# A chunked recurrence on one core: the state summed in PSUM, copied by ScalarE, and read for the queries behind the update

## The chip, the cores and the metric

One core of a Trainium2 chip runs the whole program. The metric is the device time of one execution in microseconds (us). Each kernel is executed several times and the median is given; one further execution is profiled, and its trace is what the rows below are from.

## The reference

The input x is 2048 tokens by 512 features in float32. It goes through an attention-like layer and then a feed-forward layer, each with a residual and a LayerNorm.

```python
def step(S, inp):                       # one chunk of 16 tokens, 16 heads of 32
    qi, ki, vi, ei = inp
    kh = ki @ S                         # keys read the state
    target = vi - ki
    kh_hat = (kh - mean(kh)) * rsqrt(var(kh) + EPS)
    g = w * kh_hat + b - target
    gw = g * w
    v_new = (gw - mean(gw) - kh_hat * mean(gw * kh_hat)) * rstd
    A = where(tri, qi @ ki.T, 0) * ei
    qh = qi @ S - A @ v_new             # queries read the state of before the chunk
    o = qi + ln(qh, w, b)
    S = S - (ki * ei).T @ v_new         # the state of the next chunk
    return S, o
...
x = x + layernorm(attn(layernorm(x)))   # attn: q, k, v, beta, gate projections, the scan, Wo
x = x + layernorm(ffn(layernorm(x)))    # ffn: weights rounded to fp8 values, silu(gate) * up, down
```

The scan is a chain of 128 steps; everything else can be done beside it. B and T are laid out as one sequence of 2048 tokens, so there are 128 chunks in all.

## The kernel before

The 2048 tokens are 16 tiles of 128 tokens. A tile has 8 chunks; in a chunk both halves of the heads are worked together. Every engine has its own program, and `timeline(body, prologue)` runs a prologue and then `body(t)` for t = 0 to NT + DRAIN - 1. In body(t) the scan is at tile t, the projections (`prep_...`) are made for tile t + 1, the LayerNorm of the input for t + 2, the output normalisation (`post_...`) for t - 1, the residual and second LayerNorm (`tail_...`) for t - 2, and the feed-forward layer runs in pairs of tiles behind that (`ffn_...`, `fin_...`). The order on each engine is written out by hand: for each chunk j = 0 to 7 there is scan work, then background work assigned to that j. Engines wait on semaphores, always in order.

One chunk of the scan, before:

- TensorE (`read_state`): four products `KAv[...] = bdk * SQv` (L431, "kh"), which give the keys' read of the state and, from 16 more columns, the queries against the keys. Then four products for the queries' read of the state into `QH` (L440, "qs"). Then TensorE's background of this j.
- VectorE (`scan_front`, `scan_back`): from `bn_stats` (L1140) over some ten small steps to `VX` (L1176). GpSimd gives it rho (L904, a power of two columns) on the way.
- TensorE (`write_state`): `dS[...] = bdkr * VX` (L454, "upd"), then `QH += atb * VX` (L461, "qa"), then a second piece of background.
- VectorE (`scan_state`): `S = S + dS` (L1183). This waits for upd. VectorE's background of this j stands behind it, apart from one operation that stands between VX and it.
- ScalarE: `chunk_q` (L720) puts the queries of the next chunk beside the state in `SQ`, once kh has read it; `take_qh` (L729) copies QH out. ScalarE's background stands before `take_qh`, and some behind it.

The next kh waits for `S` and for `chunk_q`. KA and dS lie in PSUM bank 0, QH in bank 1.

The feed-forward weights come in 36 blocks of 128x512 (256 KB), "units". They are rounded on VectorE in the chunks 0 to 24: `magic` (L1273, L1276), and one chunk later `shift` (L1280) and `quantize` (L1284). Chunk c takes the units c\*3//2 to (c + 1)\*3//2 - 1, so even chunks begin one unit and odd chunks two. The units are staged in three buffers, used in turn:

```python
for u in last_units(t, j):          # SP: the units that this chunk quantizes
    if u + 3 < UNITS:
        sp.wait_ge(s_quant, u + 1)
        stage(u + 3)
...
for u in last_units(t, j):          # VectorE, at the end of each chunk's background
    shift(u)
    quantize(u)
for u in units(t, j):
    magic(u)                        # waits for the landing of unit u
```

VectorE's background in the scan's chunk j, with s = t % 2, besides these: j 0 `tail_x1` (s = 1); j 1 `prep_thR`, `tail_x1` (s = 0), `ffn_f`; j 2 `post_n`, `pair_xl` (s = 1), `prep_kss`, `ffn_fl`, `x_stats`; j 3 `post_o`, `prep_qR`, `post_og`; j 4 `post_oss`, `prep_kn`, `prep_d`, `ffn_f`; j 5 `prep_kR`, `fin_y` twice (s = 1); j 6 `post_on`, `post_ogT`, `prep_bx`, `fin_stats` twice (s = 1); j 7 `prep_rR`, `prep_eta` (waits for TensorE's `prep_brow`, L419), `ffn_f`, `tail_stats`, `fin_out` twice (s = 1).

The prologue prepares tile 0 in the same order and in the same two PSUM banks as every other tile: q, k, then a wait for all eleven small tensors, v, keys turned, beta, gate, and at the end VectorE scales Wo by norm_w (four operations of 128x512).

Of the kernel before, what the change touches and what calls it, by code (L numbers as in the profile page):

```python
# [9 lines left out]
I32 = mybir.dt.int32  # L10
# [52 lines left out]

def begun(n):

    return not isinstance(n, int) or n >= 0


def build(nc, x, wq, wk, wv, wo, wbeta, wg1, wg2, norm_w, ln_w, ln_b, gate_w, up_w, down_w,
# [15 lines left out]
    with ctx:  # L85
# [11 lines left out]
        nw, gs, us = sb("nw", KD), sb("gs", MI), sb("us", MI)  # L97
# [38 lines left out]
        yb = [sb(f"yb{k}", D) for k in range(2)]  # L136
        xn2 = [sb(f"xn2{s}", D) for s in range(2)]
# [21 lines left out]
        QH = bank[1]  # L159
# [8 lines left out]
        s_setup = sem("s_setup")  # L168
# [11 lines left out]
        prep_v = Steps(sem("prep_v"), "kss qR kn d kR bx rR em er eM thR")  # L180
        prep_a = Steps(sem("prep_a"), "xnT q ksq qT g1 beta BDk rT th")
        prep_t = Steps(sem("prep_t"), "xnT q k qT v kT2 kT1 g1 beta dT gate cen brow")
        prep_g = Steps(sem("prep_g"), "kse rk qb b1")
# [3 lines left out]
        scan_t = Steps(sem("scan_t"), "kh qs upd qa")  # L187
        scan_v = Steps(sem("scan_v"), "bn p m at u g0 g1 s0 s1 t0 t1 vx S")
        scan_g = Steps(sem("scan_g"), "rho rho2 re")
        scan_a = Steps(sem("scan_a"), "qh")  # L190
# [49 lines left out]
        DRAIN = 4  # L240
# [48 lines left out]

        block = ctx.enter_context(nc.Block())  # L290

        @block.sync
        def _(sp):
            def stage(u):
                src = (gate_w, up_w, down_w)[u % 3]
                sp.dma_start(wst[u % 3][:, :], src[:, u // 3 * D:(u // 3 + 1) * D]).then_inc(s_stage[u % 3], 16)
# [3 lines left out]
            sp.dma_start(Wq[:, :].rearrange("p (k n) -> p k n", k=KD),  # L300
                         wq.rearrange("(k p) n -> p k n", p=P)).then_inc(s_wq, 16)
            for dst, src in ((Wg1, wg1), (Wb, wbeta)):
                sp.dma_start(dst[:, :].rearrange("p (k n) -> p k n", k=KD),
                             src.rearrange("(k p) n -> p k n", p=P)).then_inc(s_small, 16)
            for dst, src, s in ((Wk, wk, s_wk), (Wv, wv, s_wv)):
                sp.dma_start(dst[:, :].rearrange("p (k n) -> p k n", k=KD),
                             src.rearrange("(k p) n -> p k n", p=P)).then_inc(s, 16)
            for dst, src in ((Wg2, wg2), (nw, norm_w), (gs, gate_s), (us, up_s), (wR, ln_w), (bR, ln_b),
                             (wF, ln_wf), (bF, ln_bf)):
                sp.dma_start(dst[:, :], src).then_inc(s_small, 16)  # L310
            sp.dma_start(ds[:, :], down_s.partition_broadcast(P)).then_inc(s_small, 16)
            sp.wait_ge(norm_a.sem, norm_a.at("xn", 0))
            sp.dma_start(xt[:, :], x_t[1]).then_inc(s_x, 16)
            sp.dma_start(Wo[:, :].rearrange("p (k n) -> p k n", k=KD),
                         wo.rearrange("(k p) n -> p k n", p=P)).then_inc(s_wo, 16)
            for u in range(3):
                stage(u)

            def body(t, s, h):
# [16 lines left out]
                if s and is_pair(h - 2):  # L336
                    for k in range(2):
                        n = 2 * (h - 2) + k
                        sp.wait_ge(fin_v.sem, fin_v.at(f"out{k}", h - 2))
                        sp.dma_start(out_t[n], x1[n % 4][:, :]).then_inc(s_out[n % 4], 16)  # L340
# [6 lines left out]
        def _(pe):  # L347
# [13 lines left out]
            def prep_xnT(t):  # L361
                pe.wait_ge(norm_a.sem, norm_a.at("xn", t))
                if begun(t - 1):
                    pe.wait_ge(prep_v.sem, prep_v.at("em", t - 1))
                turn(PA[0], xn, prep_t.one("xnT"))

            def prep_q(t):
                pe.wait_ge(prep_a.sem, prep_a.at("xnT", t))
                proj(PA[0][:, :], Wq, D).then_inc(*prep_t.one("q"))

            def prep_beta(t):
                pe.wait_ge(prep_v.sem, prep_v.at("kR", t))
# [10 lines left out]
            def prep_k(t):  # L383
                pe.wait_ge(prep_a.sem, prep_a.at("q", t))
# [27 lines left out]
            def prep_cen(t):  # L412

                pe.wait_ge(prep_a.sem, prep_a.at("rT", t))
                mm(PA[0][:, :], cst[:, C_CEN:C_CEN + P], rT[:, :], start=True, stop=True).then_inc(*prep_t.one("cen"))  # L415

            def prep_brow(t):
                pe.wait_ge(prep_v.sem, prep_v.at("rR", t))
                mm(PA[0][:, 0:P], cst[:, C_REP:C_REP + P], bx[:, :], start=True, stop=True).then_inc(*prep_t.one("brow"))  # L419

            def read_state(n, j, s):

                c = NC * n + j
                if j == 0:
                    pe.wait_ge(prep_a.sem, prep_a.at("BDk", n))
# [3 lines left out]
                for gh in range(2):  # L429
                    for gp in range(2):  # L430
                        ins = mm(KAv[gp * 64:(gp + 1) * 64, gh, 0:48], bdk(s)[:, gh * NC + j, gp, :],  # L431
                                 SQv[:, 2 * gh + gp, :], start=True, stop=True, skip_group_check=True)
# [1037 lines left out]
```

## Time and profile before

| | |
|---|---|
| median of 3 runs | 997.14 us (993.86 to 998.51) |
| the profiled execution | 994.7 us |
| its span, first to last instruction | 992.9 us |
| TensorE busy | 865.5 us (87%) |
| VectorE busy | 697.9 us (70%) |
| ScalarE, GpSimd busy | 456.5 us (46%), 447.1 us (45%) |
| mean granted TensorE clock | 0.916 |

Busy time is the time that an engine's instructions cover. In the rows PE is TensorE, DVE VectorE, ACT ScalarE, POOL GpSimd and SP the queue that issues the transfers; L1183 is a line of the kernel. A buffer is named by the tensor that owns it, so that S appears as SQ, KA, QH and dS as bank, and the staging buffers as x and xn.

### The profile page before, as it was taken

How to read it: one execution, taken by the hardware profiler on the slowest of the kernel's cores; microseconds unless marked ns; L12 is line 12 of the kernel's file. 1: busy time of each engine (PE TensorE's matmuls, PEld its weight loads, DVE VectorE, ACT ScalarE, POOL GpSimd, SP SyncE). 2: the span in 40 equal slices, each digit the busy share in tenths (PEclk: the TensorE clock that was granted, in tenths of full speed). 3: DMA queues.
4: the chain of work that ended last, by engine and by line, in shares of the span. 5: the costliest groups of instructions: out<-in, count | busy, mean ns of one | idle time of the engine just before them, and what ended most of it. 6: DMA issues, size and time to landing. Idle time of an engine off the chain costs nothing.

```text
span 992.9 us, 21210 instructions
## 1 busy us (share of the span) xinstructions
PE 865.5 (87%) x7488; PEld 621.6 (63%) x7488; DVE 697.9 (70%) x2746; ACT 456.5 (46%) x1250; POOL 447.1 (45%) x828
## 2 busy tenths in 40 slices
PE   4676757677999999999999999999999999979895
PEld 2334435344667767676767676767676676767694
DVE  1477898888767777767776777767776777676442
ACT  3434324334454646464555565554556364542322
POOL 3231351533546454545463554545454545446312
PEclk9776766767999999999999999999999999989998
DMA  7011112111000001000000001000100010001000
GB/s 254 11 44 54 54 53 65 54 43 43 2 23 2 23 1 44 2 23 1 23 23 23 1 2 44 2 22 2 44 2 22 2 44 1 2 1 44 1 22 21
DMA packets 16714, 28.37 MB, mean 29 GB/s; under 512 B 3520, under 2 KB 3520, under 8 KB 16608
## 3 DMA queue, kind: packets, MB, share of 16 engines
q1 hardware_dynamic: 16608, 27.02, 8.5%
q8 instruction: 59, 0.97, 0.4%
q14 instruction: 47, 0.39, 0.1%
HBM read 22.82 MB, written 4.19 MB: 27 GB/s over the span
## 4 chain that ended last, share of the span: by engine, by line
PE 64%; DVE 20%; POOL 7%; issue 4%; ACT 2%; SPq 1%; DMA 1%; POOLq 0%; DVEq 0%; ACTq 0%
PE bank L352 14%; PE bank L489 13%; PE bank L520 8%; PE bank L473 6%; PE bank L454 5%; PE bank L461 3%; POOL rho L904 3%; PE bank L431 3%; PE bank L358 3%; PE bank L440 2%; PE bank L409 2%; PE bank L374 2%; PE bank L415 2%; DVE work L1167 2%; DVE work L1171 1%
## 5 line engine op out<-in xcount | busy, mean ns | idle before, releaser
L904 POOL TENSOR_TENSOR rho<-sy,cst 128x2 f32<-128x2 f32 x128 | 89.8, 702 | 390.6 <-DVE sy L1140 390.6
L454 PE MATMUL bank<-VX,BDkR 128*64 128x64 f32 x1024 | 61.3, 244 | 84.0 <-DVE VX L1176 83.5
L729 ACT ACTIVATE qhR<-bank 128x64 f32<-128x64 f32 x128 | 28.4, 222 | 224.9 <-PE bank L461 221.4
L454 PEld LDWEIGHTS bank<-VX,BDkR 128*64 128x64 f32 x1024 | 43.6, 145 | 137.3 <-issue 75.1
L1183 DVE TENSOR_TENSOR SQ<-SQ,bank 128x128 f32<-128x128 f32 x128 | 36.8, 288 | 94.9 <-PE bank L454 94.1
L520 PE MATMUL bank<-DW,fh 128*128 128x512 f32 x192 | 87.7, 457 | 1.9 <-DVE fl L1248 1.9
L688 ACT ACTIVATE BDkR<-kR,cst 128x128 f32<-128x128 f32 x256 | 81.1, 392 | 0.0
L520 PE MATMUL bank<-DW,fl 128*128 128x512 f32 x192 | 76.4, 398 | 0.0
L1162 DVE SCALAR_TENSOR_TENSOR work<-work,rho,rR 128x32 f32<-128x32 f32 x256 | 53.1, 249 | 31.2 <-POOL rho L904 30.5
L352 PE MATMUL bank<-Wv,xnT 128*128 128x512 f32 x128 | 66.8, 670 | 2.5 <-DVE qR L1085 2.5
L489 PE MATMUL bank<-xh,GW 128*128 128x256 f32 x384 | 66.0, 295 | 2.7 <-DVE xl L1233 2.4
L352 PE MATMUL bank<-Wq,xnT 128*128 128x512 f32 x128 | 67.3, 673 | 0.8 <-ACT xnT L623 0.8
L431 PEld LDWEIGHTS bank<-SQ,BDk 128*64 128x64 f32 x1024 | 44.6, 149 | 36.8 <-issue 28.1
L489 PE MATMUL bank<-xh,UW 128*128 128x256 f32 x384 | 66.8, 297 | 0.7 <-DVE f L1242 0.7
L985 POOL TENSOR_TENSOR fl<-f,fh 128x512 fp32r<-128x512 f32 x32 | 45.7, 1429 | 45.1 <-ACT fh L623 29.3
L473 PE MATMUL bank<-Wo,o 128*128 128x512 f32 x128 | 62.6, 634 | 2.6 <-DVE o L1215 2.6
L431 PE MATMUL bank<-SQ,BDk 128*64 128x48 f32 x1024 | 60.5, 243 | 4.4 <-DVE Wo L1396 3.1
L674 ACT ACTIVATE BDk<-bank 32x256 f32<-32x256 f32 x128 | 48.0, 375 | 34.2 <-PE bank L358 32.7
L489 PE MATMUL bank<-xl,GW 128*128 128x256 f32 x384 | 62.8, 287 | 0.0
L489 PE MATMUL bank<-xl,UW 128*128 128x256 f32 x384 | 62.8, 287 | 0.0
L1140 DVE BATCH_NORM_STATS2 sy<-bank 128x6 f32<-128x68 f32 x128 | 28.9, 226 | 47.5 <-PE bank L431 47.4
L720 ACT ACTIVATE SQ<-qT 128x64 f32<-128x64 f32 x128 | 32.3, 253 | 61.6 <-PE bank L431 61.1
(149 smaller groups left out, 2202.6 us busy)
## 6 DMA issues: line engine op xcount, KB each, us to landing
xt<-in_x SPq DMA_DIRECT2D x16, 256.0 KB, 2.7
x<-in_x SPq DMA_DIRECT2D x16, 256.0 KB, 2.9
out<-x SPq DMA_DIRECT2D x16, 256.0 KB, 2.1
x<-in_gate_w SPq DMA_DIRECT2D x12, 256.0 KB, 2.6
x<-in_up_w SPq DMA_DIRECT2D x12, 256.0 KB, 2.6
xn<-in_down_w SPq DMA_DIRECT2D x12, 256.0 KB, 2.8
Wq<-in_wq SPq DMA_DIRECT2D x1, 1024.0 KB, 8.4
Wk<-in_wk SPq DMA_DIRECT2D x1, 1024.0 KB, 10.0
```

Of the source, the lines that this page charges most:

```text
L352: ins = mm(dst, xnT[:, k * P:(k + 1) * P], W[:, k * n:(k + 1) * n], start=(k == 0), stop=(k == KD - 1))
L431: ins = mm(KAv[gp * 64:(gp + 1) * 64, gh, 0:48], bdk(s)[:, gh * NC + j, gp, :], SQv[:, 2 * gh + gp, :], start=True, stop=True, skip_group_ ...
L454: ins = mm(dS[p, e], bdkr[:, gh, j % 4, p], VX[:, e], start=True, stop=True, skip_group_check=True)
L473: ins = mm(PA[1][:, :], ogT[:, g * P:(g + 1) * P], Wo[:, g * D:(g + 1) * D], start=(g == 0), stop=(g == 3))
L489: ins = mm(b[:, q * PAIR:(q + 1) * PAIR], W[:, k * I + m * P:k * I + (m + 1) * P], part[:, k * PAIR:(k + 1) * PAIR], start=(part is xh and ...
L520: ins = mm(Y[k][:, :], part[:, q * PAIR + k * P:q * PAIR + (k + 1) * P], DW[:, m * D:(m + 1) * D], start=(m == 0 and part is fh), stop=(m ...
L674: ins = fn(bdk(s)[q, :, gp, own(h)], PA[1][p:p + 32, 256 * a:256 * a + 256].rearrange("p (m c) -> p m c", c=CH), ACT.Copy)
L688: ins = fn(bdkr[:, :, place, h * DH:(h + 1) * DH], kR[:, :].rearrange("p (gh j e) -> p gh j e", gh=2, e=DH)[:, :, js], ACT.Identity, scale ...
L904: tt(dst, src, cst[:, C_NH:C_NH + n], ALU.pow).then_inc(*one)
L985: tt(fl[:, :], f[:, :], fh[:, :].bitcast(F32), ALU.subtract).then_inc(*low_g.one("fl"))
L1162: stt(out=g2(g)[:, gh], in0=g2(u)[:, gh], scalar=rho[:, gh:gh + 1], in1=r_j[:, gh, :], op0=ALU.mult, op1=ALU.add).then_inc(*scan_v.one(f"g ...
L1183: tt(S, S, dS.rearrange("p (g e) -> p g e", e=DH), ALU.add).then_inc(*scan_v.one("S"))
```

## The change

It does these things.

1. The state is summed in PSUM: upd accumulates onto dS over all 128 chunks (only the very first clears it), `scan_state` is gone from VectorE, and ScalarE copies dS (128x128) into one of two SBUF buffers in turn (`take_S`).
2. The queries' read of the state (qs) moves from behind kh to behind upd. Both KA and QH now lie in bank 1, and kh waits for `take_qh` of the chunk before, which stands behind `take_S` on ScalarE.
3. On ScalarE `prep_q`, `prep_ksq` and `prep_th` move from before the two copies to behind them.
4. VectorE's background is dealt anew: `x_stats` from j 2 to j 1 (s = 1) or j 5 (s = 0); `tail_stats` for odd tiles and the second `fin_out` from j 7 to j 0 of the next tile; GpSimd's `tail_ra` (s = 0) from j 0 to j 1, `norm_rs` from j 3 to j 2 or j 6.
5. The units are staged in two buffers instead of three, and yb shares xn2's buffers.
6. A new prologue: k before q, beta, v and q into banks of their own, each wait for just what is needed, memsets behind the first normalisation, Wo's scaling on GpSimd, half of one copy and r's scaling on VectorE. Transfers are issued in the new order.
7. The prep stages have one semaphore for each step (`Each`), so that their order may differ. DRAIN is 5 instead of 4, for the moved `fin_out`.

```diff
-        SQ = sb("SQ", 4 * 48)
+        SQ = [sb(f"SQ{n}", 4 * 48) for n in range(2)]
...
-        wst = [x1[2], x1[3], xn2[1]]
-        wmg = [yb[0], f]
+        wst = [x1[2], x1[3]]
+        wmg = [xn2[1], f]
...
-        KA, dS = bank[0][:, 0:100], bank[0][:, 128:256]
+        dS = bank[0][:, 0:128]
+        KA, QH = bank[1][:, 0:100], bank[1][:, 128:192]
...
                     for u in last_units(t, j):
-                        if u + 3 < UNITS:
+                        if u + 2 < UNITS:
                             sp.wait_ge(s_quant, u + 1)
-                            stage(u + 3)
+                            stage(u + 2)
...
             def read_state(n, j, s):
                 pe.wait_ge(chunk_a.sem, chunk_a.at("q", c))
-                if begun(c - 1):
-                    pe.wait_ge(scan_v.sem, scan_v.at("S", c - 1))
+                if begun(c - 1):
+                    pe.wait_ge(scan_a.sem, scan_a.at("qh", c - 1))
...
             def write_state(n, j, s):
-                        ins = mm(dS[p, e], bdkr[:, gh, j % 4, p], VX[:, e], start=True, stop=True,
+                        ins = mm(dS[p, e], bdkr[:, gh, j % 4, p], VX[:, e], start=(c == 0 and gh == 0), stop=True,
                 ins.then_inc(*scan_t.one("upd"))
+                ...                                   # the four qs products, from S[c % 2]
+                ins.then_inc(*scan_t.one("qs"))
...
+            def take_S(n, j):
+                act.wait_ge(scan_t.sem, scan_t.at("upd", NC * n + j))
+                fn(S[(j + 1) % 2], dS.rearrange("p (g e) -> p g e", e=DH), ACT.Copy).then_inc(*scan_a.one("S"))
...
                     if scan:
+                        take_S(t, j)
                         take_qh(t, j, s)
...
+                    if j == 1 and prep:
+                        prep_q(t + 1)
+                    if j == 2 and prep:
+                        prep_ksq(t + 1)
...
-            def scan_state(n, j):
-                c = NC * n + j
-                dve.wait_ge(scan_t.sem, scan_t.at("upd", c))
-                tt(S, S, dS.rearrange("p (g e) -> p g e", e=DH), ALU.add).then_inc(*scan_v.one("S"))
...
             def magic(u):
-                dve.wait_ge(s_stage[u % 3], 16 * (u // 3 + 1))
+                dve.wait_ge(s_stage[u % 2], 16 * (u // 2 + 1))
...
             def prologue():                           # VectorE, the end
                 prep_eta(0, 0, Y[0])
                 prep_rR(0, 0, Y[1])
                 prep_qR(0, 0, G)
                 prep_thR(0, 0)
-                for g in range(KD):
-                    ins = ts(Wo[:, e], Wo[:, e], nw[:, g:g + 1], KAPPA, ALU.mult, ALU.mult)
```

## Rows read from the trace of the kernel before

**Rows 1.** The page, busy time, share of the span, instructions of each engine

```profile
PE 865.5 (87%) x7488; PEld 621.6 (63%) x7488; DVE 697.9 (70%) x2746; ACT 456.5 (46%) x1250; POOL 447.1 (45%) x828
```

**Rows 2.** Windows: busy us of PE, PEld, DVE, ACT, POOL, then clock, DMA

```profile
43.00:229.00 186.00, 130.72 (x1023) 82.69 (x1024) 157.23 (x557) 65.43 (x195) 61.75 (x114) 0.68 0.18 55
...
283.00:861.00 578.00, 560.52 (x5144) 405.14 (x5144) 421.11 (x1773) 308.25 (x855) 298.87 (x553) 0.99 0.05 15
...
861.00:906.00 45.00, 37.52 (x375) 30.47 (x373) 34.55 (x154) 15.79 (x45) 21.53 (x42) 0.89 0.01 1
...
906.00:993.00 87.00, 70.23 (x449) 61.51 (x448) 35.19 (x73) 24.99 (x46) 27.58 (x50) 0.92 0.07 25
```

**Rows 3.** Waits of DVE, 43 to 240 us: us in total, times, longest

```profile
DVE SQ L1183 <- PE bank L454: 14.8, 21, 2.6
...
DVE sy L1140 <- PE bank L431: 2.8, 4, 0.9
```

**Rows 4.** Waits of PE, 43 to 240 us

```profile
PE bank L454 <- DVE VX L1176: 58.3, 15, 6.2
```

**Rows 5.** Timeline of DVE in chunks 8 and 9: start, us, instruction, idle before

```profile
108.88 0.29 DVE L1183 TENSOR_TENSOR SQ<-SQ,bank 128x128 f32<-128x128 f32 x1 [0.28 <-PE bank L454]
109.08 0.68 DVE L1280 TENSOR_TENSOR x<-x,yb 128x512 f32<-128x512 f32 x1
109.80 0.69 DVE L1284 TENSOR_TENSOR UW<-x,yb 128x512 fp32r<-128x512 f32 x1
...
111.74 0.42 DVE L1273 TENSOR_SCALAR yb<-x 128x512 int32<-128x512 int32 x1
...
116.55 0.69 DVE L1284 TENSOR_TENSOR GW<-x,yb 128x512 fp32r<-128x512 f32 x1
...
117.96 0.42 DVE L1273 TENSOR_SCALAR yb<-xn 128x512 int32<-128x512 int32 x1
```

**Rows 6.** Timeline of SP in chunk 9

```profile
117.27 0.33 SPq L296 DMA_DIRECT2D x<-in_gate_w  x1
```

**Rows 7.** DMA issues: KB each, median us from issue to landing

```profile
x<-in_gate_w SPq DMA_DIRECT2D x12, 256.0 KB, 2.6
...
xn<-in_down_w SPq DMA_DIRECT2D x12, 256.0 KB, 2.8
```

**Rows 8.** Timeline of ACT in chunk 10 (j 2 of tile 1)

```profile
120.65 0.60 ACT L650 ACTIVATE xn_dv_rT<-bank 128x512 f32<-128x512 f32 x1 [3.85 <-PE bank L352]
122.29 0.22 ACT L729 ACTIVATE qhR<-bank 128x64 f32<-128x64 f32 x1 [1.05 <-PE bank L461]
```

**Rows 9.** The chain that ended last, in the prologue: start, us, what

```profile
13.13 4.72 DMA ds<-in_down_s
```

**Rows 10.** Timeline of the prologue and of the first chunk

```profile
10.35 5.28 PE L352 MATMUL bank<-Wq,xnT 128*128 128x512 f32 x8 [0.78 <-ACT xnT L623]
...
23.31 2.91 POOL L904 TENSOR_TENSOR rk<-kss,cst 128x16 f32<-128x16 f32 x1
...
41.63 1.63 DVE L1396 TENSOR_SCALAR Wo<-Wo,nw 128x512 f32<-128x512 f32 x4
...
44.13 0.24 DVE L1140 BATCH_NORM_STATS2 sy<-bank 128x6 f32<-128x68 f32 x1 [0.87 <-PE bank L431]
```

**Rows 11.** Timeline of POOL and DVE behind the scan

```profile
918.07 1.30 POOL L980 TENSOR_TENSOR o<-o,wK 128x512 f32<-128x512 f32 x1
...
918.09 1.82 DVE L1248 TENSOR_TENSOR fl<-f,fh 128x512 fp32r<-128x512 f32 x1
```

**Rows 12.** Timeline of PE, tile 6 j 0 and tile 7 j 3

```profile
392.75 0.45 PE L454 MATMUL bank<-VX,BDkR 128*64 128x64 f32 x8 [1.39 <-DVE VX L1176]
...
463.98 0.45 PE L454 MATMUL bank<-VX,BDkR 128*64 128x64 f32 x8 [1.30 <-DVE VX L1176]
```

**Rows 13.** Timeline of DVE, tile 6 j 7 to tile 7 j 0

```profile
438.48 0.29 DVE L1121 TENSOR_TENSOR work<-bank,cst 128x128 f32<-128x128 f32 x1 [1.40 <-PE bank L419]
...
440.85 0.20 DVE L1140 BATCH_NORM_STATS2 sy<-bank 128x6 f32<-128x68 f32 x1
```

More of the change, by code:

```diff
@@ L61, in at, with __init__, one @@
         return len(self.names) * n + self.names.index(name) + 1
+class Each:
+    def __init__(self, sem, stage, names):
+        self.sems = {name: sem(f"{stage}_{name}") for name in names.split()}
+    def one(self, name):
+        return self.sems[name], 1
+    def at(self, name, n):
+        return self.sems[name], n + 1
 def begun(n):
@@ L135, in build @@
         f = sb("f", D)
-        yb = [sb(f"yb{k}", D) for k in range(2)]
-        xn2 = [sb(f"xn2{s}", D) for s in range(2)]
+        xn2 = yb = [sb(f"xn2{s}", D) for s in range(2)]
         norms = ("p", "a", "f", "y0", "y1")
@@ L179, in build @@
         norm_a = Steps(sem("norm_a"), "xn")
[L180 to L183, printed above, removed]
+        prep_v = Each(sem, "prep_v", "kss qR kn d kR bx rR em er eM thR")
+        prep_a = Each(sem, "prep_a", "xnT q ksq qT g1 beta BDk rT th")
+        prep_t = Each(sem, "prep_t", "xnT q k qT v kT2 kT1 g1 beta dT gate cen brow")
+        root_g = Steps(sem("root_g"), "kse rk")
+        prep_g = Each(sem, "prep_g", "qb b1")
         diag_a = Steps(sem("diag_a"), "q0 q1")
@@ L332, in body @@
                     for u in last_units(t, j):
-                        if u + 3 < UNITS:
+                        if u + 2 < UNITS:
                             sp.wait_ge(s_quant, u + 1)
-                            stage(u + 3)
[L336 to L340, printed above, removed]
+                            stage(u + 2)
+                if is_pair(h - 3 + s):
+                    p, k = h - 3 + s, 1 - s
+                    n = 2 * p + k
+                    sp.wait_ge(fin_v.sem, fin_v.at(f"out{k}", p))
+                    sp.dma_start(out_t[n], x1[n % 4][:, :]).then_inc(s_out[n % 4], 16)
             timeline(body, lambda: None)
@@ L614, in prologue @@
-                pe.wait_ge(s_setup, 4)
+                pe.wait_ge(norm_a.sem, norm_a.at("xn", 0))
+                turn(PA[0], xn, prep_t.one("xnT"))
+                pe.wait_ge(*prep_a.at("xnT", 0))
+                pe.wait_ge(s_wk, 16)
+                proj(PA[1][:, :], Wk, D).then_inc(*prep_t.one("k"))
+                pe.wait_ge(s_early, 16 * 2)
+                for k in range(KD):
+                    ins = mm(Y[0][0:DG, 0:P], Wg1[:, k * DG:(k + 1) * DG], xnT[:, k * P:(k + 1) * P],
+                             start=(k == 0), stop=(k == KD - 1))
@@ new lines, in prologue @@
+                ins.then_inc(*prep_t.one("g1"))
+                proj(Y[0][:, P:P + H], Wb, H).then_inc(*prep_t.one("beta"))
+                pe.wait_ge(s_wv, 16)
+                proj(Y[1][:, :], Wv, D).then_inc(*prep_t.one("v"))
+                pe.wait_ge(s_wq, 16)
+                proj(G[:, :], Wq, D, (0, 1))
+                pe.wait_ge(*prep_v.at("kn", 0))
+                turn(PA[0], kn, prep_t.one("kT2"))
+                turn(PA[1], kn, prep_t.one("kT1"))
+                pe.wait_ge(*prep_v.at("d", 0))
@@ new lines, in prologue @@
+                turn(U4, dv, prep_t.one("dT"))
+                proj(G[:, :], Wq, D, (2, 3)).then_inc(*prep_t.one("q"))
+                pe.wait_ge(*prep_v.at("bx", 0))
+                mm(Y[0][:, 0:P], cst[:, C_REP:C_REP + P], bx[:, :], start=True, stop=True).then_inc(*prep_t.one("brow"))
+                pe.wait_ge(*prep_a.at("rT", 0))
+                mm(Y[1][:, :], cst[:, C_CEN:C_CEN + P], rT[:, :], start=True, stop=True).then_inc(*prep_t.one("cen"))
+                pe.wait_ge(*prep_a.at("q", 0))
@@ L616, in _ @@
+                turn(G, qtok, prep_t.one("qT"))
+                pe.wait_ge(s_small, 16 * 6)
+                for m in range(4):
+                    ins = mm(U4[:, m * P:(m + 1) * P], Wg2[:, m * P:(m + 1) * P], g1T[:, :], start=True, stop=True)
+                ins.then_inc(*prep_t.one("gate"))
+                pe.wait_ge(s_half, 1)
+                pe.wait_ge(s_mask, 2)
             timeline(body, prologue)
@@ L1312, in body @@
                         prep_rR(t + 1, o)
-                    if scan:
-                        scan_state(t, j)
-                    if j == 0 and tail and s:
-                        tail_x1(t - 2)
+                    if j == 0:
+                        if tail and s:
+                            tail_x1(t - 2)
+                        if tail and not s:
+                            tail_stats(t - 2)
+                        if not s and is_pair(h - 3):
+                            fin_out(h - 3, 1)
                     if j == 1:
```

335 lines of the change are left out of this document (177 added, 158 removed).

## The prediction

> **What bounds the kernel now.** I read the page's busy times first: TensorE 87%, VectorE 70% [rows 1]. Such a share is a mean over stages, so the windows came next [rows 2], and they show four. From 43 to 229 us (tiles 0 to 2, while the weights are rounded) VectorE is busy 157 of 186 us and TensorE 131 at a clock of 0.68: VectorE bounds. From 283 to 861 us (tiles 4 to 14) TensorE is busy 560.5 of 578 us: it bounds, and only 17.5 us can be won there. From 861 to 906 us (tile 15, nothing left to project) TensorE has 7.5 us without work: the chain through the chunk bounds. From 906 us on there is no scan. Ahead of all this stands a prologue of 44 us. The waits agree: between 43 and 240 us VectorE waits 14.8 us for upd in front of the state's add and 2.8 us for kh in front of `bn_stats` [rows 3], while TensorE waits 58.3 us for VX [rows 4]. The timeline of one even and one odd chunk then shows VectorE's instructions back to back [rows 5].
>
> **The change, part by part, against the profiled span of 992.9 us.**
>
> *Staging in two buffers.* In which chunk is a unit loaded, and in which is it needed? With two buffers unit u + 2 is issued when unit u is quantized. In an odd chunk VectorE quantizes one unit, 3k, and then begins 3k + 1 and 3k + 2; the transfer of 3k + 2 is issued only at the end of that same quantize. In an even chunk it quantizes 3k + 1 and 3k + 2 and begins 3k + 3, whose transfer is issued behind the first of these. Before, with three buffers, each had a whole chunk's time. Quantize starts at 116.55, the transfer is issued at 117.27, 0.72 later [rows 5, 6], and lands 2.6 to 2.8 us after its issue [rows 7]; with 0.04 for the wake, `magic` can start some 3.4 us behind the quantize's start. Without the wait it would start sooner: in the odd chunk the unit in question is the second begun, at 117.96, 1.41 behind the quantize; in the even chunk it is the one begun at 111.74, 1.94 behind the quantize at 109.80 [rows 5]. So VectorE stands 2.05 us in each odd chunk (down or the like, 2.7 to 2.8) and 1.42 in each even one. Units 2, 5, ... 35 are twelve odd cases, 3, 6, ... 33 eleven even ones: 12 x 2.05 + 11 x 1.42 = **+40.2**. It lies on VectorE, in order, right in front of the next `scan_front`. Bounds: 0 if VectorE would wait for kh there anyway, but that wait is 2.8 us in all [rows 3]; 23 x 2.1 = 48 at most.
>
> *`scan_state` gone.* VectorE no longer waits for upd in front of its background. In tiles 0 to 2 that frees the 14.8 and 2.8 us of waits and, from start to start, 0.20 us for each of 24 adds [rows 3, 5]: 22.4. Against that stand three things that are late next. `prep_kss` needs `prep_ksq`, which ScalarE now does behind upd, qs, qa and both copies. Before, it started at 120.65, ahead of `take_qh` at 122.29 [rows 8], and kss followed the add without a wait. Now it starts after it, and kss some 2 us later than VectorE can take it: three tiles, 6 us. `prep_eta` needs brow, which comes behind upd, qs and qa: VectorE reaches it an add earlier and it comes the length of qs later, some 0.8 us, three times, 2.4. And chunk 0, with only one `magic` behind VX, waits 2.2 us for the next kh. Together -22.4 + 10.6 = **-12**. Bounds: everything freed, -28.8, the whole idle time of VectorE in this stretch [rows 2]; nothing, 0.
>
> *Prologue.* Before, k's product waits till 17.9 us for the last of eleven small tensors [rows 9], and v's waits in one bank for k's; GpSimd's power over 16 columns is 2.91, and Wo's scaling, 1.63, is the last thing ahead of the scan [rows 10]. Now k starts where q did, at 10.35, and ends near 15.6, as q did with 5.28; square, sum and power take 0.6, 0.7 and 3.1 (here and behind, each step has the length that the same step has in the prologue before), so rk is there at 20.3 while beta's and v's products end near 21. Then kn 22.5, keys turned 24.1, rest of q 26.5, brow and cen 28.1, q turned 28.7, four copies and the queries' columns on ScalarE 30.6. Two sets of diagonal copies (1.67 and 1.28) and tanh follow at 34.1, thR's turn on VectorE 34.8, then `bn_stats`, which was at 44.13 [rows 10]: **-9**. GpSimd's four products of 512 columns at 1.3 [rows 11] run from 23 to 28.7, beside this. Bounds -5 (a landing 4 us later, each step behind it) and -12.
>
> *Steady tiles.* Here TensorE waits in four chunks of a pair of tiles: about 1.4 and 0.6 in the even tile, 0.1 and 1.3 in the odd one (two of them in [rows 12]). All come from VectorE's background being late at the end of a chunk. At j 7 it isn't the add that makes it late: VectorE waits 1.4 us for brow at 438.48, then works till `bn_stats` at 440.85 [rows 13], and brow follows TensorE's order as before. What helps in front of even tiles is the moved `tail_stats` and `fin_out` (0.8 + 0.65): `bn_stats` 1.4 earlier. At j 2 the new wait for ksq makes VectorE late by about 1 us for j 3, against 1.3 and 2.2 before. But qs no longer fills TensorE's time until VX, so in each chunk where TensorE waits for VX its 0.35 us is added. Per pair: j 0 even -1.0, j 3 even 0, j 0 odd +0.35, j 3 odd -0.75: -1.4. 5.5 pairs: -7.7, and -1.3 for stretches of low clock that followed the longest waits: **-9**. Elsewhere qs is only moved within TensorE's own work. Bounds: -17.5, all of the idle time [rows 2], and +6 if the qs term comes alone.
>
> *The copies.* A ScalarE copy of 64 columns is 0.22 us and 512 columns are 0.60 [rows 8], so 128 take about 0.28. Behind upd come qs, qa (0.35 each) and TensorE's second background (0.5 to 1.4 in full tiles), so both copies are hidden. Where there is none, in tiles 0 to 2 and tile 15, kh now waits 0.3 for `take_qh`, hidden in the former by VectorE.
>
> *Tile 15.* Here TensorE waits for VX in five or six chunks; each grows by qs 0.35 and some by the copy's 0.3, less what VectorE saves: **+2**, between 0 and 4. Behind it: the same work, 0; the moved `fin_out` waits for the same things.
>
> *A lock between VectorE and GpSimd.* At 918.09 a VectorE operation with two SBUF inputs takes 1.82 us, beside GpSimd's 1.30 of 512 columns that began 0.02 before it [rows 11]. GpSimd's big operations wait for VX and used to run beside the add's wait; now they start with VectorE's background. At j 6 `prep_bx` would stand about 0.7 us, in each of 12 tiles. I count 0, since VectorE there has about that much time to spare before TensorE's next kh; on the path it is 8 us. The Trainium skill (SBUF — State Buffer, section "SBUF: two separate sides") says that the pair is held exclusively for a whole instruction and the loser blocks; by that rule the sum has these 8 us wherever the two meet on the path, and the trace agrees with the rule in this one case: 1.82 where such operations take 0.68 or 0.69 [rows 5].
>
> Sum: +40.2 - 12 - 9 - 9 + 2 = +12.2; 992.9 becomes 1005.1, and 994.7 with what lies around it 1006.9. The runs' median is 2.4 above the profiled execution, which would give 1009.3. I take **1008**.
>
> **Rivals.** (a) *The landing is hidden.* VectorE's wait for a unit replaces a wait that it would have for TensorE, so that the 40 us cost little. For it: TensorE's low clock in tiles 0 to 2 makes its work long, 131 of 186 us [rows 2]. Against: TensorE waits 58 us for VX there [rows 4]. Fully hidden it gives 968. It decides once the waits cost under 28 us, 1.2 for each of 23. Chance 0.13. (b) *The steady tiles give all their idle time back*, because ksq and the rest come in time, and VectorE's relief is nearer 20 than 12: -8 and -8, 992. Chance 0.19. (c) *The new copies or GpSimd hold the chain*: ScalarE does its background before `take_S`, and a late copy delays kh; at 0.3 us in half the chunks, or the 8 us of the lock and a cold TensorE during the longer waits, +10 to +14: 1020. Chance 0.13. (d) My case, 1000 to 1016: 0.55.
>
> **How the numbers follow.** 0.5% is 5 us, about what a measurement of this kernel can tell from no change. Slower by more than that: (c) and nearly all of (d): 0.66. Same: half of (b) and some of (d), 0.15. Faster: (a), and the rest of (b), 0.19. For 8 in 10 the range must take in (b) and (c) and leave (a) out: 985 to 1021; my own case alone is 1000 to 1016.
>
> **What would show it.** VectorE idle in front of `magic` (L1273 before), ended by a DMA, 23 times and some 40 us in all; if it is under 20, the first step is wrong. The first `bn_stats` near 35 us. Window of tiles 0 to 2 about 28 us longer. VectorE waiting for ksq about 1.5 us at j 2. TensorE's waits for VX in tiles 4 to 14 about 14 to 17 us still; if they are near 0, (b). ScalarE's `take_S` starting later than 0.3 us behind upd in more than a few chunks, with kh behind it: (c).

## The result and the profile after

The changed kernel takes 1000.3 us (median of 14 runs, 998.2 to 1003.3), the kernel before, in the same sessions, 995.1 (14 runs): a ratio of 1.0051, 95% interval 1.0038 to 1.0063. The change costs 0.5%. I had predicted slower, by 1.1% (997.1 to 1008, or 10.9 us; the medians differ by 5.2). The profiled execution took 1002.5 us, its span 1000.7.

The table goes by five stretches. Their borders are the first `bn_stats` and the first kh product of tiles 3, 4 and 15, read from the timelines of both kernels (before: 44.13, 229.27, 282.95 and 861.24).

| stretch | before | after | difference | predicted |
|---|---|---|---|---|
| start to first `bn_stats` | 44.1 | 34.6 | -9.6 | -9 |
| from there to tile 3 (weights rounded) | 185.1 | 212.9 | +27.8 | +40.2 - 12 = +28.2 |
| tile 3 | 53.7 | 55.7 | +2.0 | 0 |
| tiles 4 to 14 | 578.3 | 565.9 | -12.4 | -9 |
| tile 15 and behind the scan | 131.7 | 131.7 | 0.0 | +2 |
| span | 992.9 | 1000.7 | +7.8 | +12.2 |

The borders after, from TensorE's timeline (start, us, instruction); the second and third have 565.9 us between them:

```profile
247.49 0.44 PE L453 MATMUL bank<-SQ,BDk 128*64 128x48 f32 x8
...
303.17 0.44 PE L453 MATMUL bank<-SQ,BDk 128*64 128x48 f32 x8
...
869.08 0.44 PE L453 MATMUL bank<-SQ,BDk 128*64 128x48 f32 x8
```

The page after, busy times, to be read against [rows 1]: VectorE has lost 26 us of work (the 128 adds), ScalarE has 26 more, and TensorE has 7 less.

```profile
PE 858.4 (86%) x7480; PEld 616.3 (62%) x7480; DVE 672.1 (67%) x2623; ACT 482.3 (48%) x1370; POOL 449.7 (45%) x832
```

The windows after, in the columns of [rows 2]:

```profile
34.50:247.50 213.00, 133.55 (x1018) 83.25 (x1018) 152.31 (x533) 71.45 (x220) 59.61 (x114) 0.65 0.16 46
303.50:869.00 565.50, 552.98 (x5140) 399.86 (x5136) 402.21 (x1685) 327.55 (x943) 298.91 (x553) 1.00 0.05 16
869.00:916.00 47.00, 37.96 (x391) 30.95 (x390) 34.62 (x150) 18.22 (x53) 23.01 (x47) 0.89 0.01 2
916.00:1001.00 85.00, 68.08 (x432) 59.63 (x430) 32.85 (x69) 24.33 (x46) 26.84 (x45) 0.92 0.08 25
```

In tiles 0 to 2 no engine is near full any more: VectorE is busy 152 of 213 us, TensorE 134, at a granted clock of 0.65 (1 is 2.4 GHz, 0.5 is 1.2 GHz; a figure between them is a mean over time). VectorE's waits over the whole span, the four ended by a landing and three others, and below them those of TensorE from 34.5 to 247.5 us:

```profile
DVE sy L1197 <- PE bank L453: 90.7, 68, 3.6
DVE work L1178 <- PE bank L441: 35.0, 15, 2.7
DVE kss L1126 <- ACT xn_dv_rT L690: 32.0, 15, 2.8
...
DVE f L1329 <- DMA x<-in_down_w: 13.4, 6, 3.3
DVE xn L1329 <- DMA x<-in_down_w: 11.7, 6, 2.1
...
DVE f L1329 <- DMA x<-in_gate_w: 8.5, 6, 1.8
DVE xn L1329 <- DMA x<-in_gate_w: 6.7, 5, 1.4
```

```profile
PE bank L467 <- DVE VX L1233: 71.3, 18, 7.9
PE bank L453 <- ACT qhR L769: 6.0, 12, 1.5
```

The four DMA lines add up to 40.3 us in 23 waits; 40.2 in 23 was forecast. One wait of 2.2 us falls in tile 3, the other 38.1 us in tiles 0 to 2. (TensorE's wait for VX was 58.3 us in [rows 4], which reach into tile 3, and 52.2 in tiles 0 to 2 alone, against the 71.3 here.) VectorE's timeline in an odd and in an even chunk shows how each arises:

```profile
117.02 0.69 DVE L1340 TENSOR_TENSOR GW<-x,xn 128x512 fp32r<-128x512 f32 x1
117.63 0.42 DVE L1329 TENSOR_SCALAR f<-x 128x512 int32<-128x512 int32 x1
...
120.41 0.43 DVE L1329 TENSOR_SCALAR xn<-x 128x512 int32<-128x512 int32 x1 [1.89 <-DMA x<-in_down_w]
...
127.54 0.69 DVE L1340 TENSOR_TENSOR UW<-x,f 128x512 fp32r<-128x512 f32 x1
...
130.87 0.43 DVE L1329 TENSOR_SCALAR f<-x 128x512 int32<-128x512 int32 x1 [1.31 <-DMA x<-in_gate_w]
```

From the quantize that frees the buffer to the `magic` that waits for it are 3.39 and 3.33 us; "some 3.4" was forecast.

### The profile page after: what moved, and what is told of

Its sections match the earlier page's. It is cut to its first block, busy times and chain, and to the rows that moved or that the text cites. A ratio compares the mean times of both kernels' runs of the same rounds, so it can differ in the third digit from the quotient of the medians.

```text
span 1000.7 us, 21166 instructions
## 1 busy us (share of the span) xinstructions
PE 858.4 (86%) x7480; PEld 616.3 (62%) x7480; DVE 672.1 (67%) x2623; ACT 482.3 (48%) x1370; POOL 449.7 (45%) x832
## 4 chain that ended last, share of the span: by engine, by line
PE 61%; DVE 18%; POOL 7%; DMA 7%; ACT 4%; issue 3%; POOLq 0%; SPq 0%; ACTq 0%; DVEq 0%
PE bank L374 15%; PE bank L511 11%; PE bank L542 8%; PE bank L495 5%; PE bank L467 5%; PE bank L481 4%; POOL rho L952 3%; DMA x<-in_down_w 3%; PE bank L380 3%; DMA x<-in_gate_w 3%; PE bank L453 2%; PE bank L474 2%; DVE work L1224 2%; PE bank L437 1%; DVE work L1228 1%
## 5 line engine op out<-in xcount | busy, mean ns | idle before, releaser
L762 ACT ACTIVATE SQ<-bank 128x128 f32<-128x128 f32 x128 | 35.2, 275 | 229.9 <-PE bank L467 229.7
L467 PEld LDWEIGHTS bank<-VX,BDkR 128*64 128x64 f32 x1024 | 44.0, 146 | 151.0 <-issue 81.4
L374 PE MATMUL bank<-Wk,xnT 128*128 128x512 f32 x128 | 60.9, 620 | 2.3 <-DMA Wk<-in_wk 2.3
```

The costliest lines, as they stand in the source:

```text
L374: ins = mm(dst, xnT[:, k * P:(k + 1) * P], W[:, k * n:(k + 1) * n], start=(k == 0), stop=(k == KD - 1))
L467: ins = mm(dS[p, e], bdkr[:, gh, j % 4, p], VX[:, e], start=(c == 0 and gh == 0), stop=True, skip_group_check=True)
```

## The experiments

Eleven kernels ran. e1, e3, e5, e7 and e9 are built on the changed kernel, e2 and e11 on the one before; e4 joins e1 and e3, and e6, e8 and e10 are built on e4. e1 to e4 were timed on one chip, e5 to e8 on a second and e9 to e11 on a third, each time beside the kernel before (994.7 to 996.0 there), and the ratio is to that. The last three columns are stretches of the table above, from the timeline of each kernel's one profiled execution.

| kernel | median | ratio (95%) | first `bn_stats` to tile 3 | tile 3 | tiles 4 to 14 |
|---|---|---|---|---|---|
| before | 995 | 1 | 185.1 | 53.7 | 578.3 |
| after | 1000.3 | 1.0051 (1.0038 to 1.0063) | 212.9 | 55.7 | 565.9 |
| e1 three buffers | 971.3 | 0.9764 (0.9739 to 0.9790) | 184.5 | 53.0 | 566.0 |
| e2 before, two buffers | 1028.4 | 1.0337 (1.0318 to 1.0357) | 218.6 | 56.2 | 575.2 |
| e3 ksq early | 993.4 | 0.9977 (0.9963 to 0.9990) | 210.3 | 55.3 | 558.0 |
| e4 = e1 + e3 | 960.6 | 0.9656 (0.9638 to 0.9673) | 184.4 | 53.1 | 558.1 |
| e5 deal undone | 1025.8 | 1.0316 (1.0300 to 1.0331) | 209.8 | 56.0 | 595.7 |
| e9 = e5 + ksq early | 1002.3 | 1.0065 (1.0050 to 1.0080) | 209.3 | 56.1 | 572.1 |
| e7 state's copy doubled | 1001.6 | 1.0068 (1.0051 to 1.0085) | 212.4 | 55.9 | 566.0 |
| e6 = e4 + eta behind | 949.9 | 0.9546 (0.9518 to 0.9574) | 177.6 | 52.2 | 555.1 |
| e8 = e4 + fillers | 953.4 | 0.9588 (0.9571 to 0.9605) | 175.1 | 52.5 | 558.2 |
| e10 = e6 + fillers | 944.7 | 0.9477 (0.9454 to 0.9501) | 172.5 | 52.0 | 555.1 |
| e11 before + eta, fillers | 986.2 | 0.9893 (0.9856 to 0.9931) | 185.5 | 53.1 | 568.6 |

**What a staging buffer is worth (e1, e2).** The edit on the changed kernel; e2 is the reverse of it on the kernel before.

```diff
-        wst = [x1[2], x1[3]]
+        wst = [x1[2], x1[3], sb("w3", D)]
...
-                        if u + 2 < UNITS:
+                        if u + 3 < UNITS:
                             sp.wait_ge(s_quant, u + 1)
-                            stage(u + 2)
+                            stage(u + 3)
```

> The changed kernel with one more staging buffer, so that a unit is loaded a chunk ahead again; nothing else differs. My theory: VectorE's waits for landings in tiles 0 to 2 are on the path, so nearly all of them come off: the time falls by 35 to 42 us against the changed kernel, to about 962, and the stretch of tiles 0 to 2 is 35 to 40 us shorter. Rival (the landing replaces another wait): it falls by less than 15 us, and VectorE waits for kh or for k's squares instead.

> The kernel before with two staging buffers instead of three, that part of the change alone. My theory: slower by 30 to 40 us; a little under the sum of the waits, since waits for upd in front of the state's add are swallowed. Rival: by less than 12 us.

e1 measured 29 us less than the changed kernel (35 to 42 expected), e2 32 to 34 more than the kernel before (30 to 40 expected). So the two buffers explain the whole loss and more, but at a price of 28 to 33 us in tiles 0 to 2, not 40. Where did the rest go? VectorE's waits in e1, first `bn_stats` to tile 3:

```profile
DVE sy L1197 <- PE bank L453: 8.9, 8, 2.1
DVE kss L1126 <- ACT xn_dv_rT L690: 6.3, 3, 2.8
...
DVE work L1178 <- PE bank L441: 4.2, 2, 2.4
...
DVE xn_dv_rT L1159 <- PE bank L374: 1.3, 1, 1.3
```

With the landings gone, VectorE meets TensorE: these four are 20.7 us, while the changed kernel has 12.0 there for kss, brow and kh (6.7 + 2.7 + 2.6), so 8.7 of the 38.1 us there only changed their name. That leaves 29.4, and the stretch is 28.4 us shorter. In e2 the same: 38.7 us of landing waits, but the wait for upd fell from 14.5 to 9.6 and that for kh from 2.8 to 0.9. Its first three lines:

```profile
DVE yb L1273 <- DMA x<-in_down_w: 12.0, 6, 2.1
DVE f L1273 <- DMA x<-in_down_w: 10.2, 5, 2.2
DVE SQ L1183 <- PE bank L454: 9.6, 16, 3.6
```

The more telling comparison is e1 with the kernel before. Both have three buffers, and e1 has no add on VectorE; yet tiles 0 to 2 take 184.5 us against 185.1. The relief of 12 us that I had counted is not there: the 20.7 us above stand where 14.5 for upd and 4.8 for kh, brow and kss stood. VectorE is busy 6 us less (151.0 against 157.0) and idle 5 us more.

**ksq behind the copies (e3, e4).** `prep_ksq` goes back ahead of `take_S` at j 2:

```diff
                         if s and is_pair(h - 1):
                             pair_xh(h - 1)
+                        if prep:
+                            prep_ksq(t + 1)
...
-                    if j == 2 and prep:
-                        prep_ksq(t + 1)
```

> The changed kernel with the squares of k (prep_ksq) back in front of ScalarE's two copies at j 2. My theory: VectorE's late start at j 3 (1.04 us) goes, and with it TensorE's wait of 0.64 in each of the tiles 4 to 14, 7 us, and a wait of 1.5 to 2 us in each of the tiles 0 to 2: 9 to 13 us faster than the changed kernel. Rival: the later state copy delays kh by the 0.6 us of the squares in every tile, so that nothing or half of it is won: 0 to 5 us.

> Both together: one more staging buffer and the squares of k early. If the two are separate terms their gains add: some 48 us faster than the changed kernel, about 950. If with the landings gone another wait bounds tiles 0 to 2, the sum is short by more than 5 us.

In the changed kernel the steady tiles have this in each tile (VectorE, tile 8 j 2, and TensorE's wait behind it):

```profile
529.07 0.69 DVE L1126 TENSOR_REDUCE kss<-xn_dv_rT 128x16 f32<-128x512 f32 x1 [2.16 <-ACT xn_dv_rT L690]
...
532.87 0.45 PE L467 MATMUL bank<-VX,BDkR 128*64 128x64 f32 x8 [0.64 <-DVE VX L1233]
```

By the medians e3 takes 7 us less, between the theory (9 to 13) and the rival (0 to 5). Its profiled execution was 2.3 us under its own median, so the stretches show more: 7.9 less in tiles 4 to 14, where TensorE's waits for VX fall from 9.9 to 2.6 us, and 2.6 in tiles 0 to 2. On three buffers (e4) the steady gain is the same 7.9 and the one in tiles 0 to 2 is nil: kss's wait falls from 6.3 to 2.6 us and the time stays (184.5, 184.4). So in tiles 0 to 2 it is not this wait that bounds either. e4 missed its expectation of some 950, but its gain, 39.7 us, is not under the sum of what e1 and e3 bring alone, 29.0 and 6.9: most of the miss is e1's.

**VectorE's background (e5, e9).** `x_stats` back to j 2, `tail_stats` and both `fin_out` to j 7, GpSimd's `tail_ra` and `norm_rs` and the output's transfers as before:

```diff
                     if j == 2:
...
+                        if norm:
+                            x_stats(t + 2)
...
                     if j == 7:
...
-                        if post and not s:
+                        if post:
                             tail_stats(t - 1)
                         if fin:
                             fin_out(h - 2, 0)
+                            fin_out(h - 2, 1)
```

> The changed kernel with VectorE's background dealt as before: x_stats at j 2, tail_stats and both fin_out at j 7, GpSimd's tail_ra and norm_rs where they were. Theory: the deal takes 1.45 us from VectorE ahead of chunk 0 of an even tile, and one pair of steady tiles went from 104.6 to 103.0 us mainly by this; undone, the wait for VX in that chunk comes back, some 1.4 us a pair: about +8 us in tiles 4 to 14, 1008. Rival: the steady tiles owe their gain to the add that is gone, and TensorE hides the rest: within 2 us of 1000.

> The changed kernel (two buffers) with VectorE's background dealt as before and prep_ksq ahead of take_S again: of the change there stay the state in PSUM, qs behind the update, the two buffers and the prologue. With the deal undone alone the time was 1025.8, with a wait of 1.4 us at j 3 and a lower clock behind it in each steady tile. Theory: the late ksq made that wait; with it early the wait is under 0.5 us, the clock holds, and tiles 4 to 14 take about as long as in the kernel before, 575, against 595.7: about 1003. Rival: x_stats at j 2 is too much there with or without ksq, and half of the loss stays: 1012 to 1018.

e5 costs 25 us by the medians, 29.8 in tiles 4 to 14 (and some 5 less elsewhere): three times what I expected. TensorE's waits for VX there grow from 9.9 to 25.6 us, which is half of it. The other half is its clock, a mean of 0.97 where it was 1.00. TensorE's wait in tile 8 j 3 of e5, and windows over the chunks 2, 3 and 4 of that tile (last columns: granted clock, DMA):

```profile
541.69 0.45 PE L467 MATMUL bank<-VX,BDkR 128*64 128x64 f32 x8 [1.44 <-DVE VX L1230]
```

```profile
529.00:537.00 8.00, 8.00 (x80) 4.74 (x80) 4.20 (x20) 3.51 (x10) 3.73 (x9) 1.00 0.00 1
537.00:544.20 7.20, 5.76 (x64) 5.24 (x62) 6.14 (x22) 4.00 (x14) 4.57 (x8) 0.92 0.01 3
544.20:551.40 7.20, 7.20 (x47) 3.87 (x46) 4.97 (x19) 2.45 (x8) 2.90 (x6) 0.84 0.00 0
```

Chunk 4 has no idle time, and takes 7.1 us, since part of it is worked at 1.2 GHz. The same chunk of the changed kernel, behind a wait of 0.64 us:

```profile
534.90:541.00 6.10, 6.10 (x46) 3.29 (x44) 4.97 (x19) 2.44 (x8) 2.31 (x4) 1.00 0.00 1
```

This wait of 1.44 us was thus paid a second time, by about 1.5 us (0.5 in chunk 3, 1.0 in chunk 4), and the one of 0.64 us was not. The Trainium skill (TensorE: Matmul & The Clock Gate, "HAM oscillation — how this bites in real kernels") describes a kernel that pays such a fall again in every round of its loop, because each round has a wait, there of some 3 to 5 us. The trace of e5 agrees that the fall comes back: 0.92 and 0.84 here, chunks 3 and 4 as long in tiles 10 and 11 (7.4 and 7.1, 7.3 and 7.3 us), and a stretch at 1.2 GHz behind j 3 in nine of the eleven tiles. But it comes behind shorter waits, and the length of a wait does not decide it alone. In j 0 of the same tile 8, TensorE waits longer and keeps its clock:

```profile
522.23 0.45 PE L467 MATMUL bank<-VX,BDkR 128*64 128x64 f32 x8 [1.66 <-DVE VX L1230]
```

```profile
522.20:537.00 14.80, 14.77 (x130) 9.14 (x132) 8.60 (x37) 8.30 (x24) 8.69 (x14) 1.00 0.06 19
```

None of e5's five waits of 1.65 and 1.66 us in j 0 is followed by a fall. The kernel before has eleven waits of 1.3 to 1.6 us in tiles 4 to 14 and three falls; e2, with the same eleven waits, has one; e9 has five waits of 1.66 to 1.67 and one fall. What sets j 3 of e5 apart stays open.

e9 came out as its theory had it: with ksq early, the wait at j 3 is 0.36 to 0.56 us, waits for VX are 14.4 us in all, and tiles 4 to 14 take 572.1. So late ksq costs 7.9 us beside the new deal and 23.6 beside the old one (595.7 - 572.1), and the undone deal costs 14.1 beside early ksq (572.1 - 558.0) and 29.8 beside late. Each edit hides a part of what the other costs.

**The copies (e7).** One more copy of the state, into a buffer that nobody reads, ahead of `take_S`'s own:

```diff
+                fn(scr[:, :], dS, ACT.Copy)
                 fn(S[(j + 1) % 2], dS.rearrange("p (g e) -> p g e", e=DH), ACT.Copy).then_inc(*scan_a.one("S"))
```

> The changed kernel with one more ScalarE copy of the 128 columns of the state, into a buffer that nobody reads, ahead of take_S in every chunk: 0.28 us more from upd to kh, 128 times. Theory (the copies are hidden in tiles 0 to 14, on the path in tile 15): +1 to +3 us, about 1002. Rival (ScalarE's copies hold the chain): +0.28 in at least half of the chunks, +18 to +36, about 1025.

ScalarE's groups in e7 (busy us, mean ns; then its idle time ahead of them). The added copies are 35.3 us by themselves, and 21.5 of ScalarE's busy time (503.8 against 482.3), since the second copy of a pair starts 0.17 us behind the first; so the test delays the state by 0.17 us, 128 times.

```profile
L763 ACT ACTIVATE scr<-bank 128x128 f32<-128x128 f32 x128 | 35.3, 276 | 230.4 <-PE bank L468 230.2
L764 ACT ACTIVATE SQ<-bank 128x128 f32<-128x128 f32 x128 | 34.6, 271 | 0.0
```

The time went from 1000.3 to 1001.6, inside the intervals, and no stretch of the first table grew by more than 0.3 us. That is in the range expected, but not by the way that was given for it, tile 15, which did not grow. The copies are hidden, as counted, and rival (c) is out in its first part.

**Why VectorE's relief came to nothing (e6, e8, e10, e11).** Two suspects stand in tiles 0 to 2: brow, for which VectorE waits at j 7 with the rounding of weights queued behind it, and TensorE's clock. The first edit moves `prep_eta` on VectorE; the second puts products on TensorE ahead of `write_state` ("fillers"), in eight chunks.

```diff
-                        if prep:
-                            prep_eta(t + 1, o)
...
                     for u in units(t, j):
                         magic(u)
+                    if j == 7 and prep:
+                        prep_eta(t + 1, o)
```

```diff
+                    if t < 3 and j in (0, 3, 5) and t + j:
+                        for k in range(4 if j < 5 else 3):
+                            mm(G[:, :], ident, Wk[:, 0:D], start=True, stop=True)
```

> Three buffers and prep_ksq early (960.6 us), and at j 7 prep_eta behind VectorE's other work instead of ahead of it. In the kernel that it is built on VectorE waits 8.5 us for brow in tiles 0 to 2 and about 2.3 us in each later one. Theory: the wait is VectorE's loss in tiles 0 to 2, and goes: -5 to -8 us there and 0.3 a tile after them, 950 to 953. Rival: TensorE at its low clock is as late, and VectorE waits for kh instead: 958 to 961.

> Three buffers and prep_ksq early (960.6 us), and in tiles 0 to 2, where TensorE waits 4 to 6 us for VX (chunks 0, 3 and 5), 4, 4 and 3 more products of 512 columns into a bank that nobody uses there, ahead of the wait; their results are not used. Theory: VectorE's freed time came to nothing in tiles 0 to 2 because TensorE works there at the low clock (0.69 granted); with the fillers it is granted over 0.9, and the chunks in which TensorE sets the pace (1, 4, 6, 7) shorten by a fifth: -12 to -18 us, about 946. Rival: VectorE alone bounds tiles 0 to 2 (169 of 208 us busy), and the fillers end after VX in some chunks: 0 to +5 us, about 962.

> Three buffers, prep_ksq early, prep_eta behind VectorE's other work at j 7 (949.9 us) and the products that fill TensorE's waits in tiles 0 to 2 (alone they brought 7 us on top of 960.6). Theory (two causes apart, brow's wait on VectorE and TensorE's low clock): both gains add up, 942 to 944. Rival (both remove the same wait, since brow is late because TensorE works at the low clock): 948 to 950.

> The kernel before (three buffers, VectorE's add) with the same two edits: prep_eta behind VectorE's other work at j 7, and the fillers in tiles 0 to 2. Theory: the fillers raise the clock in tiles 0 to 2 there too, and upd, which VectorE's add waits for, comes sooner: -8 us; eta behind gives little, since the add's wait stands in front of it anyway: -2; 985. Rival: in the kernel before VectorE sets the pace of tiles 0 to 2 whatever TensorE's clock: 993 to 997. If it falls as far as it did with the state in PSUM (-18), the new order of the state is worth no more than prologue and deal.

e6 brings 11 us by the ratios, as its theory had it: 6.8 in tiles 0 to 2, 3.0 in tiles 4 to 14. e8 brings 7, where 12 to 18 were expected, at a clock of 0.85 where over 0.9 was: 9.3 in tiles 0 to 2, some of it given back behind tile 14 (131.8 us from tile 15 on, against 128.8 in e4's execution). The windows of e8 and of e10 in tiles 0 to 2, against a clock of 0.68 in e1 and in e4:

```profile
32.50:207.50 175.00, 141.21 (x1074) 80.53 (x1074) 151.15 (x533) 71.38 (x220) 60.40 (x114) 0.85 0.20 60
```

```profile
34.40:206.90 172.50, 143.39 (x1076) 82.48 (x1077) 152.44 (x537) 71.55 (x220) 60.41 (x114) 0.83 0.21 61
```

Both edits gain, and they overlap: together 11.9 us in tiles 0 to 2, where 6.8 and 9.3 would add up to 16. e10 lies between its two theories, nearer to the first. e11 hit its number for the wrong reason: all of its gain is in tiles 4 to 14 (568.6), where no fillers stand and TensorE's waits for VX fell from 16.7 to 9.5 us, with one fall of the clock instead of three. Tiles 0 to 2 did not move, as the rival had it for them, although the clock there rose from 0.69 to 0.80. VectorE waits more for upd there, 17.9 us instead of 14.5:

```profile
45.00:230.50 185.50, 150.75 (x1073) 86.84 (x1070) 156.74 (x557) 65.30 (x195) 61.61 (x114) 0.80 0.19 55
```

```profile
DVE SQ L1186 <- PE bank L454: 17.9, 16, 3.7
```

Some of this wait is the edits' own doing. In j 0 of tile 1 of e11 TensorE begins the fillers late, behind a wait for `prep_eta` (1.31 us), and they run on for 3 us after VX is there; upd stands behind them, and VectorE's add behind upd (VX ends at 107.68):

```profile
105.67 5.19 PE L575 MATMUL bank<-Wk,cst 128*128 128x512 f32 x8
110.80 0.45 PE L454 MATMUL bank<-VX,BDkR 128*64 128x64 f32 x8
```

```profile
107.39 0.29 DVE L1179 TENSOR_TENSOR VX<-work,re 128x128 f32<-128x128 f32 x1
...
111.30 0.29 DVE L1186 TENSOR_TENSOR SQ<-SQ,bank 128x128 f32<-128x128 f32 x1 [3.02 <-PE bank L454]
```

In tile 2 upd is 2.7 us late in the same way. So e11 does not show what the higher clock alone is worth beside the add.

With these two edits on both sides, tiles 0 to 2 take 172.5 us with the state in PSUM (e10) and 185.5 with the add (e11), 13 us apart. This is not the 12 us that I had counted. Those had 6 taken off for a late kss and 2.4 for brow, and e10 has ksq early and eta behind; without them the count would have been some 20. And the two kernels also differ in the deal (1 us in this stretch, by e9 against e3) and ksq, and upd is held up by fillers in both (3.4 and 1.1 us in j 0 of tiles 1 and 2 of e10). That freed VectorE time is worth something once other waits are gone is shown; how much of it is the state's is not. e10, at 944.7 us, is the fastest kernel here, 5.2% under the kernel before.

Not tried: qs in front of VX again with the state in PSUM. What the moved qs costs is therefore not known apart from the rest.

## Why the prediction came out as it did: what held, and which steps failed

The direction held, and so did the time, 1000.3 in a range of 985 to 1021. The size of the change did not: 10.9 us forecast, 5.2 measured. The sum of the terms was +12.2, the spans differ by 7.8. The steps that failed in this sum are the steady tiles' term (-9, measured -12.4, and in it the 1.3 us for low clock, measured as about 5) and tile 15's (+2, measured 0); tile 3, set to 0, took 2.0 of it back. The other 2.6 us between spans and medians are the profiled execution's. The two largest terms were each off by some 7 to 11 us and made up for it in the sum.

- **Staging, +40.2.** The waits were right to 0.1 us and in number, the price of this term by itself was not: 28.4 (against e1) to 33.5 (e2) in tiles 0 to 2, and 2.5 to 2.7 in tile 3. The step that failed is the bound "0 if VectorE would wait for kh there anyway, but that wait is 2.8 us in all". On the kernel before a landing covers waits for upd too, which that bound leaves out (4.9 us of them in e2, and 1.9 for kh: 40.2 - 6.8 = 33.4). And once the add is gone, the waits that a landing covers are those of the new kernel (8.7 us in e1).
- **`scan_state` gone, -12.** Mis-sized: -0.7 with three buffers (e1), -5.7 with two (212.9 against e2's 218.6). With two buffers the time given back was right: the 12.0 us for kss, brow and kh, less 2.0 that VectorE waited for kss and brow before, are 10.0, and 10.6 was forecast. The time freed was not: in e2 the landings have already taken over a part of the waits, and 9.6 + 0.9 + 4.8, some 15, is left of the 22.4; 15.3 - 10.0 = 5.3 fits the 5.7. With three buffers the freed time is right (some 22 us) and some 19 are given back (20.7 less 2.0), by waits for TensorE. I named kss, brow and chunk 0; what I left out is that TensorE, at 0.68, sets the pace of several chunks. The 6.8 us that I took too much for staging I also took too much off here, since it is the same overlap seen from both sides, and the sum came out at +28.2 against +27.8. The prediction did not argue this; in that respect the agreement is luck.
- **Prologue, -9.** -9.6. `bn_stats` was forecast 0.7 us behind the start of thR's turn:

```profile
33.94 0.71 DVE L1142 STREAM_TRANSPOSE thR<-q_kn_th 128x512 f32<-128x512 f32 x1 [3.07 <-ACT q_kn_th L940]
34.57 0.20 DVE L1197 BATCH_NORM_STATS2 sy<-bank 128x6 f32<-128x68 f32 x1
```

- **Steady tiles, -9.** -12.4. Of this, TensorE's waits for VX are 6.8, near the 7.7 forecast (16.7 before, 9.9 after; the sign to look for, 14 to 17 left, did not fit that sum). Most of the rest is clock: I gave it 1.3, while the kernel before lost about 5.1 us (a mean of 0.991 over 578.3 us, three falls) and the changed kernel none (1.000). This part is not firm. e2 has the same work and the same waits there (16.8 us), one fall instead of three, a mean of 0.997, and takes 575.2; against that execution the changed kernel is 9.3 us faster. And the net hid larger parts: the new deal is worth 14 us (e9 against e3) and the late ksq costs 7.9.
- **Tile 3, 0.** +2.0: it is the last landings, since e1 has 53.0 there.
- **Tile 15 and behind, +2.** 0.0: from the first kh to the last upd of tile 15 it is +0.6 (45.5 and 46.1 us), and -0.6 behind it. The added qs and copy, 0.35 and 0.3 in five or six chunks, did not come through; what covered them no run shows.
- **Copies, 0.** Shown by e7. The first form of rival (c), 0.3 us in half the chunks, would have been 19 us and not the 10 to 14 given.
- **Lock of VectorE and GpSimd, 0.** At j 6 the two do meet. VectorE's operation with two SBUF inputs was first, by 0.16 us, and kept its length; GpSimd's took 1.66 us (1.65 or 1.66 at j 6 of every tile from 3 on). At j 0, where the VectorE operation that starts 0.16 us ahead of it has one SBUF input, it takes 1.27 or 1.28. `prep_bx` waits 0.59 for what is behind it, in even tiles ahead of a wait of 1.30 for kh; in odd tiles there is no such wait, but TensorE does not wait for VX at j 7 in either, so it is off the path:

```profile
447.59 0.69 DVE L1263 TENSOR_TENSOR o<-o,ro 128x512 f32<-128x512 f32 x1
...
449.61 0.36 DVE L1135 TENSOR_TENSOR bx<-bt,cst 128x64 f32<-128x64 f32 x2 [0.59 <-POOL bt L980]
```

```profile
447.75 1.66 POOL L1033 TENSOR_TENSOR fl<-f,fh 128x512 fp32r<-128x512 f32 x1 [1.19 <-DVE VX L1233]
```

  The same section of the Trainium skill that the prediction drew on (SBUF — State Buffer, "SBUF: two separate sides") has the loser as the one that came second, and the trace agrees.
- **From the span to the median.** The sum missed the span by 4.4 us. As much again came from taking over an offset: the profiled execution of before was 2.4 under the median of three runs, but 0.35 under that of fourteen, and that of after is 2.2 above its own. One profiled execution says nothing of a median to better than some 2 us.

Of the rivals, (a) had a part of the truth, a quarter of the wait hidden, but stayed above its own point of decision, 28 us. (b), a time of 992, needed ksq in time: with it early (e3), 993.4; its other condition, a relief of VectorE near 20, did not come. (c), GpSimd or the copies on the path, was not seen; the colder TensorE that it also names was there, 0.65 against 0.69 in tiles 0 to 2, and no run separates its price.

## What to carry to other kernels

Count a new wait as a wait, but price it only against what the same engine would wait for next in the new kernel; and do the same with freed time, above all where two engines are near the bound. A free engine is worth nothing while another wait stands in front of its work: move work that waits for a slow producer (`prep_eta`) behind work that doesn't. A buffer less between SyncE and its consumer costs a wait wherever the next use follows the release sooner than a new load can: here 3.4 us from the last use's start to the next use, so that 1.4 and 1.9 us between them became waits of 2.1 and 1.4.

## What the runs showed of the hardware

A short wait of TensorE can be paid twice, and need not be. In e5 nine waits of 1.43 to 1.55 us were each followed by a stretch at the low level that cost as much again (1.5 us in tile 8), while five of 1.65 and 1.66 us in the same trace, and all waits of 0.64 us in the changed kernel, left the granted clock at 1.00. In the kernel before three of eleven waits of 1.3 to 1.6 us were followed by such a stretch, in e2 one of the same eleven. So a trace with a few of them is a sample.

In tiles 0 to 2 of e4, 51 us of TensorE's idle time (184.4 less 133.6) went with a granted clock of 0.68; filling a part of it with products whose result is not used (e8) gave 0.85 and took 7 us off, although TensorE had more to do. Beside the add (e11) the same products gave 0.80 and took nothing off there, in part because they outlast VX.

And GpSimd, not VectorE, can be the one that is held when their operations of 512 columns meet: 1.66 us in place of 1.27, behind a VectorE operation with two SBUF inputs.
